# Attention and experts in one kernel: one key row block copied by ScalarE, fewer zero fills, and weight and row-part transfers issued from ScalarE's queue

## The chip, the cores and the metric

One core of a Trainium2 chip runs the whole program. The metric is the device time of one execution in microseconds, taken as the median over several runs. The engines are named as in the profile: PE (TensorE), DVE (VectorE), ACT (ScalarE), POOL (GpSimd) and SP (SyncE, which here only issues DMAs). SPq and ACTq are the DMA-issuing instructions of SP and ACT.

## The reference

A layer normalised input goes through latent attention (16 heads of 8 content and 32 rotary columns, 16 batches of 256 tokens) and, beside it, through a mixture of 8 experts with the two best taken, and a shared expert. Both results are added to the input.

```
x  = L0_attn_x                      # 16 x 256 x 128, float32
xn = layernorm(x)
kv = rmsnorm(xn @ W_kv) * g_kv;  q_c = xn @ W_q
k  = [kv @ W_kdec, rope(xn @ W_krope)];  v = kv @ W_vdec
q  = [q_c @ W_qdec, rope(q_c @ W_qrope)]           # 16 heads x 40 columns
attn = softmax(causal(q k^T / sqrt(40))) v @ W_o
probs = softmax(xn @ Wg);  two best of 8, renormalised
ffn  = sum over the two of (silu(xn @ W1[e] + b1[e]) @ W2[e] + b2[e]) * weight
       + 0.1 * (silu(xn @ Ws1 + bs1) @ Ws2 + bs2)
out  = x + attn + ffn
```

## The kernel before, in words

**Two phases.** In the first, `run_turns` runs turns b = -3 to 16 on every engine, each of `STEPS` = 16 steps. A turn works on several batches at once: it projects and turns batch b+2, takes the row maxima of b and b+1, the final scores, exponentials and values of b, and finishes b-1. What is done at which step stands in hand-written tables (`PROJ_AT`, `TURNED_AT`, `MROWS_AT`, `PV_AT` and others), so each engine's order is fixed, and semaphores tie the engines together. Turns 1, 5, 9 and 13 also hold a router group of eight tiles, whose work lies mostly on DVE. In the second phase `expert_out`, `hidden` and their partners run 31 passes of 512 rows: two shared ones, 23 routed blocks, six shared ones.

**High and low parts.** Products are taken in float32r with each operand split in a rounded high part and the rest. The queries and keys of a head are therefore stacked three times in `QK`: 3 blocks of `D` = 40 partitions. `part_heads` (ACT, L802) copies a turned bank to `heads_high` (keys: steps 15, 0, 2 and 3), `take_low` (DVE, L1099) writes the low part, and SP's `restack` (L482) copies both by DMA, 40 partitions at a time, to the right block of `QK`: for each batch 2 sides x 3 head groups x 3 blocks = 18 copies, all at L494. Key group 0 is wanted first, by `scores_for_max` of the next batch's head 0 (PE L1529, at step 9).

**Row maxima.** `put_max` (ACT, L821 and L823) copies the turned maxima of eight heads to `mT` and places them by a small DMA in two more partitions of `QK`. It is issued at step 3 for heads 0 to 7, which `head_scores` (PE L1439) begins at step 6, and at step 11 for heads 8 to 15, begun at step 14.

**Expert weights.** In turns 0 to 8 (`weights_at`) one expert's weights a turn are split by POOL (`split_weights`, steps 8 and 11) and then, from SP's queue, stored in two DMAs of 512 KB (L517), and the next ones are loaded in two of 256 KB (L476, L477). SP also stores each batch's turned and split rows, `xn_parts`, 256 KB (L502). SP's `turn` is in this order: rows of b+2, `restack` of b+1 (keys 0 and 1, queries 2, keys 2), weights, `restack` of b+2 (queries 0 and 1).

**Fills.** After the turns, SP clears 512 rows behind each expert's last row, and 7 more blocks that stand for unused routed blocks: `FILLS` = 15 DMAs of 256 KB (L566), then waits for them and for the scattered rows before it loads block rows (L549). SP gets there while the other engines are still in turn 15.

## Time and profile before

| | |
|---|---|
| runs | 743.53 us median of 3 (740.61 to 744.3) |
| profiled execution | 746.28 us, span 744.1 us |
| PE, PEld busy | 633.1, 511.8 us |
| DVE, ACT, POOL busy | 568.2, 391.5, 356.8 us |
| mean granted TensorE clock | 0.944 of 2.4 GHz |

The span is from the first to the last instruction; 2.2 us lie around it. Issuing a DMA is not counted as busy. A turn is told below by POOL's instruction at L742, which runs once a turn at its step 1: the stretch called turn b begins with it. In the rows by stretch stand, for each engine, busy us and (x) instructions in the order PE, PEld, DVE, ACT, POOL, then the granted TensorE clock as a share of 2.4 GHz (1.00 is that level, 0.50 would be 1.2 GHz), the busy share of the 16 DMA engines and GB/s.

### The profile page before, as it was taken

Reading aid. Unit: us, or ns where it says so; the run is one execution under the profiler, and the core shown is the slowest. Engines: PE = TensorE matmul, PEld = TensorE weight load, DVE = VectorE, ACT = ScalarE, POOL = GpSimd, SP = SyncE. Lnnn points to the kernel's source line nnn. Section 1 sums busy time; section 2 is a strip of 40 time slices with the busy share of each in tenths; the row PEclk is TensorE's granted clock in tenths of the full one; section 3 lists DMA queues with packets and bytes.
Section 4 is the critical chain, followed back from the end, with each engine's and each line's share of the span. In section 5 each row is a group of like instructions: output and inputs, shape, how many; then the busy total and the mean of one; then the engine's idle time right before and its main releaser. Section 6 shows DMA issues by size and latency. Waiting matters only on the chain.

```text
span 744.1 us, 14766 instructions
## 1 busy us (share of the span) xinstructions
PE 633.1 (85%) x4646; PEld 511.8 (69%) x4646; DVE 568.2 (76%) x1456; ACT 391.5 (53%) x842; POOL 356.8 (48%) x460
## 2 busy tenths in 40 slices
PE   2668878989887888988799998777799999999995
PEld 1457657767666766766677776665578888888884
DVE  5667798867688877678978878883757777789896
ACT  1323535535453554554455655433477777777773
POOL 7526454775754667466355455332300000457673
PEclk9877999989998999999999999988989999999998
DMA  7344655656566565655444555458625877889753
GB/s 195 111 161 162 205 171 194 210 186 202 185 207 202 168 197 183 219 201 178 130 156 168 165 173 173 130 159 257 210 94 174 257 249 247 265 288 307 223 173 86
DMA packets 66285, 141.66 MB, mean 190 GB/s; under 512 B 9204, under 2 KB 34849, under 8 KB 66209
## 3 DMA queue, kind: packets, MB, share of 16 engines
q1 hardware_dynamic: 61005, 131.36, 54.7%
q0 software_dynamic: 4096, 8.40, 4.1%
q10 hardware_dynamic: 1108, 0.97, 0.4%
q8 instruction: 38, 0.62, 0.3%
q14 instruction: 38, 0.31, 0.1%
HBM read 47.30 MB, written 29.88 MB: 104 GB/s over the span
## 4 chain that ended last, share of the span: by engine, by line
PE 51%; DVE 15%; POOL 10%; issue 9%; DMA 8%; SPq 5%; ACT 2%; POOLq 0%; DVEq 0%; ACTq 0%
PE bank L1692 9%; DMA QK<-mT 5%; PE bank L1710 5%; POOL QK L778 4%; PE bank L1440 4%; PE bank L1515 3%; PE bank L1456 3%; PE bank L1529 3%; SPq L494 3%; PE bank L1532 3%; PE bank L1442 3%; PE bank L1714 3%; DVE mx L1089 3%; DVE rot L1064 2%; PE bank L1563 2%
## 5 line engine op out<-in xcount | busy, mean ns | idle before, releaser
L1089 DVE TENSOR_REDUCE mx<-bank 128x3 f32<-128x384 f32 x256 | 141.8, 554 | 76.5 <-PE bank L1532 74.3
L834 ACT ACTIVATE prob<-bank 128x384 f32<-128x384 f32 x256 | 125.2, 490 | 134.7 <-PE bank L1442 132.9
L675 POOL TENSOR_TENSOR rot<-rot,t 128x512 f32<-128x512 f32 x64 | 82.1, 1283 | 138.6 <-DVE t L1079 138.5
L778 POOL DMA_INDIRECT QK<-expert_outs,out_at x64 | 65.6, 1025 | 139.3 <-DMA expert_outs<-prob 121.0
L1529 PE MATMUL bank<-QK 120*128 120x256 f32 x256 | 97.8, 382 | 31.8 <-issue 21.5
L1383 DVE TENSOR_TENSOR QK<-vaug,QK 128x512 fp32r<-128x512 f32 x124 | 86.5, 699 | 40.8 <-ACT QK L930 38.2
L1440 PE MATMUL bank<-QK 122*128 122x256 f32 x256 | 88.3, 345 | 0.0
L1439 PE MATMUL bank<-QK 122*128 122x128 f32 x256 | 76.1, 297 | 10.2 <-DMA QK<-mT 9.8
L758 POOL DMA_INDIRECT expert_rows<-xn,place_of x64 | 67.5, 1055 | 32.7 <-PE bank L1442 22.4
L1515 PE MATMUL bank<-ident,rot 128*120 128x128 f32 x384 | 69.5, 295 | 13.4 <-DVE heads_low L1099 8.1
L1529 PEld LDWEIGHTS bank<-QK 120*128 120x128 f32 x256 | 54.5, 213 | 36.4 <-issue 24.1
L811 ACT ACTIVATE heads_high<-bank 120x384 fp32r<-120x384 f32 x96 | 47.1, 494 | 58.3 <-PE bank L1515 51.2
L1532 PE MATMUL bank<-mask_qk,identb 128*128 128x256 bf16 x256 | 76.5, 299 | 0.0
L1442 PE MATMUL bank<-identb,mask_qk 128*128 128x256 bf16 x256 | 75.3, 294 | 0.0
L1099 DVE TENSOR_TENSOR heads_low<-bank,heads_high 120x384 fp32r<-120x384 f32 x96 | 52.8, 553 | 20.8 <-ACT heads_high L811 19.4
L1692 PE MATMUL bank<-heads_high,wb 128*128 128x512 f32 x276 | 68.6, 397 | 0.0
L924 ACT ACTIVATE vaug<-bank,xn 128x512 f32<-128x512 f32 x92 | 63.0, 687 | 2.5 <-PE bank L1692 0.5
L1515 PEld LDWEIGHTS bank<-ident,rot 128*120 128x120 f32 x384 | 47.0, 147 | 24.4 <-DVE heads_low L1099 11.0
L1439 PEld LDWEIGHTS bank<-QK 122*128 122x128 f32 x256 | 51.3, 200 | 16.8 <-DMA QK<-mT 13.5
L1530 PE MATMUL bank<-QK 120*128 120x128 f32 x256 | 59.3, 232 | 0.0
L1692 PEld LDWEIGHTS bank<-heads_high,wb 128*128 128x128 f32 x276 | 50.1, 188 | 9.3
L1530 PEld LDWEIGHTS bank<-QK 120*128 120x128 f32 x256 | 52.4, 205 | 0.1
(229 smaller groups left out, 1465.1 us busy)
## 6 DMA issues: line engine op xcount, KB each, us to landing
QK<-heads_high SPq DMA_DIRECT2D x96, 200.0 KB
wb<-weight_parts SPq DMA_DIRECT2D x35, 512.0 KB, 4.7
QK<-heads_high SPq DMA_DIRECT2D x48, 240.0 KB
QK<-heads_low SPq DMA_DIRECT2D x48, 200.0 KB
weight_parts<-wb SPq DMA_DIRECT2D x18, 512.0 KB, 5.8
QK<-queries_high SPq DMA_DIRECT2D x32, 200.0 KB
rot<-expert_rows SPq DMA_DIRECT2D x23, 256.0 KB, 4.2
expert_outs<-prob SPq DMA_DIRECT2D x23, 256.0 KB, 4.5
```

The lines of the kernel that those rows point to most:

```text
L778: nc.gpsimd.indirect_dma_start(out=gy[:, t, k, :], out_offset=None, in_=outs_d[0:READY[q] * SLOTS, :], in_offset=bass.IndirectOffsetOnAxis ...
L834: act_f(prob[:, h % P_SLOTS, :], ST_PS[h % 2][:, P:4 * P], ACT.Exp, scale=SCALE).then_inc(s_exp, 1)
L1089: V.tensor_reduce(mx[:, 0:3, h], B_PS[bank_of(k)][:, 0:3 * P].rearrange("p (a c) -> p a c", a=3), AX.X, ALU.max).then_inc(s_bfree[bank_of( ...
L1383: V.tensor_tensor(aparts[:, m % 2, 1, c, :], act[c], high, ALU.subtract).then_inc(s_alo, 1)
L1439: mm(ps[:, P:T], k[:, P:T], q[:, P:T], start=True, stop=False, skip_group_check=True)
L1440: mm(ps[:, T:2 * T], k[:, 0:P], q, start=False, stop=False, skip_group_check=True)
L1442: mm(diag, mask_qk[:, :], identb[:, :].unsqueeze(1).to_broadcast([P, 2, P]), start=False, stop=True, skip_group_check=True).then_inc(s_st, 1)
L1515: ins = nc.tensor.transpose(B_PS[bank_of(k)][0:KQ, g * P:(g + 1) * P], rows[:, at:at + KQ], ident[:, :])
L1529: mm(ps[:, 0:T], q[:, P:T], kk, start=True, stop=False, skip_group_check=True)
L1530: mm(ps[:, T:T + P], q[:, 0:P], kk[:, 0:P], start=False, stop=False, skip_group_check=True)
L1532: mm(diag, identb[:, :], mask_qk[:, :].unsqueeze(1).to_broadcast([P, 2, P]), start=False, stop=True, skip_group_check=True).then_inc(s_bfi ...
L1692: ins = mm(banks[c][:, :], w[:, part * F + c * P:part * F + (c + 1) * P], xT[m % 2][:, a, :], start=(i == 0), stop=(i == 2))
```

## The change

Four edits.

1. Block 0 of key group 0 is no longer copied by DMA. ACT writes it itself behind each of the four key copies of `part_heads` (steps 15, 0, 2, 3): it waits for its own copy and copies 40 partitions x 384 elements from `heads_high` to `QK`. `restack` of key group 0 then issues two DMAs, the high one and the low one. PE waits for `s_kd` as well.
2. The stores and loads of expert weights and the store of the row parts are issued from ACT's queue: stores at steps 12 and 15, loads at step 13 and at step 1 of the next turn, row parts at step 4, each behind everything else of its step.
3. Unused routed blocks read row 0 onwards in place of cleared rows of their own, so that 8 fills are left of 15. For it DVE has one more small instruction in `list_blocks`.
4. Before the fills SP waits until the last batch's second half of maxima is placed (`s_mrow[1]`).

```diff
+W_STORE_AT = {12: 0, 15: 1}
+W_LOAD_AT = {13: (0, 0), 1: (1, 1)}
+SEND_STEP = 4
...
-FULL = 2 * TILES * P // SLOTS
-ROWS = E * CAP + (NB - FULL) * SLOTS
-FILLS = E + NB - FULL
+ROWS = E * CAP
...
-                rows_of = ((0, high), (1, high), (2, low)) if side == "q" else ((0, high), (2, high), (1, low))
-                for row, part in rows_of:
-                    if i == 0 and row == rows_of[0][0]:
-                        sp.wait_ge(s_hi, raw_no(beta, 2 * n + 1, 1) + 1)
-                    if i == 0 and row == rows_of[2][0]:
+                rows_of = {"q": (0, 1, 2), "k": (0, 2, 1) if i else (2, 1)}[side]
+                if i == 0:
+                    sp.wait_ge(s_hi, raw_no(beta, 2 * n + 1, 1) + 1)
+                for row in rows_of:
+                    if i == 0 and row == rows_of[-1]:
                         sp.wait_ge(s_bfree[bank_of(k)], FREE_NO[k])
+                    part = low if row == rows_of[-1] else high
                     sp.dma_start(QK[row * D:(row + 1) * D, beta % 2, n, heads[0]:heads[-1] + 1, :].bitcast(F32),
-                                 part[i * D:(i + 1) * D, 0:len(heads), :].bitcast(F32)).then_inc(stacked(beta, side)[0][i], 16)
+                                 part[i * D:(i + 1) * D, 0:len(heads), :].bitcast(F32)).then_inc(stacked(beta, side, i)[0], 16)
...
-                if known(b + 2):
-                    sp.wait_ge(s_xh, b + 3)
-                    sp.wait_ge(s_xl, b + 3)
-                    sp.dma_start(parts_d[:, :, (b + 2) * T:(b + 3) * T].bitcast(F32),
-                                 xhl[:, par, :, :].bitcast(F32)).then_inc(s_xst[par], 16)
...
-                e = weights_at(b)
-                if e is not None:
-                    sp.wait_ge(s_whi, 2 * (e + 1))
-                    sp.wait_ge(s_wlo, 2 * (e + 1))
-                    for part in range(2):
-                        sp.dma_start(w_d[e, :, part, :].bitcast(F32), w_split[part][:, :].bitcast(F32)).then_inc(s_wst, 16)
-                    if e + 1 < NE:
-                        load_raw(e + 1)
...
+            sp.wait_ge(s_mrow[1], 16 * B)
+            for i in range(E):
...
+                if side == "k":
+                    heads = slice(half * TG // 2, (half + 1) * TG // 2)
+                    at_least(sc, s_st, (beta - 2) * H + HEADS_OF[0][-1] + 1)
+                    sc.wait_ge(s_hi, raw_no(beta, order, half) + 1)
+                    act_f(QK[0:D, beta % 2, 1, heads, j * P:(j + 1) * P], hs[0:D, 1, heads, j * P:(j + 1) * P],
+                          ACT.Copy).then_inc(s_kd, 1)
+            def store_weights(e, part):
+                sc.wait_ge(s_whi, 2 * e + part + 1)
+                sc.wait_ge(s_wlo, 2 * e + part + 1)
+                sc.dma_start(w_d[e, :, part, :].bitcast(F32), w_split[part][:, :].bitcast(F32)).then_inc(s_wst, 16)
+            def load_weights(e, part):
+                sc.wait_ge(s_wlo, 2 * e - 1 + part)
+                if part == 0:
+                    sc.dma_start(w_raw[:, 0:F], W1[e] if e < E else Ws1).then_inc(s_wl, 16)
+                else:
+                    sc.dma_start(w_raw[:, F:2 * F].rearrange("p (c h) -> p c h", c=FC),
+                                 (W2[e] if e < E else Ws2).rearrange("(c p) h -> p c h", p=P)).then_inc(s_wl, 16)
+            def send_parts(b, par):
+                sc.wait_ge(s_xh, b + 1)
+                sc.wait_ge(s_xl, b + 1)
+                sc.dma_start(parts_d[:, :, b * T:(b + 1) * T].bitcast(F32), xhl[:, par, :, :].bitcast(F32)).then_inc(s_xst[par], 16)
...
+                    if known(b + 2) and s == SEND_STEP:
+                        send_parts(b + 2, par)
+                    e = weights_at(b)
+                    if e is not None and s in W_STORE_AT:
+                        store_weights(e, W_STORE_AT[s])
+                    if s in W_LOAD_AT:
+                        back, part = W_LOAD_AT[s]
+                        e = weights_at(b - back)
+                        if e is not None and e + 1 < NE:
+                            load_weights(e + 1, part)
...
-                    steps.add(V.memset(shift[:, SEGS:SEGS + 1], float(E * CAP - FULL * SLOTS)))
+                    steps.add(V.memset(shift[:, SEGS:SEGS + 1], 0.0))
...
+                    steps.add(V.scalar_tensor_tensor(out=seg, in0=seg, scalar=float(SEGS), in1=block_no, op0=ALU.is_lt,
+                                                     op1=ALU.mult))
...
+                            pe.wait_ge(*stacked(beta, side, i))
+                if h == 0:
+                    pe.wait_ge(s_kd, 4 * (beta + 1))
```

## Rows read from the trace of the kernel before

**Rows 1.** Busy time by stretch: turns 1, 3+4, 5, 6, 7+8, 9, 11.

```profile
86.07:121.82 35.75, 28.25 (x237) 22.50 (x237) 31.02 (x87) 15.19 (x38) 16.16 (x22) 0.90 0.58 189
149.57:211.88 62.31, 54.29 (x456) 43.61 (x456) 44.08 (x123) 30.32 (x75) 39.00 (x51) 0.92 0.60 198
211.88:247.84 35.96, 28.26 (x237) 23.36 (x237) 31.65 (x87) 15.45 (x39) 19.80 (x26) 0.91 0.59 190
247.84:276.55 28.71, 25.05 (x228) 20.04 (x228) 22.23 (x62) 15.11 (x38) 19.37 (x27) 1.00 0.59 190
276.55:337.57 61.02, 53.09 (x456) 41.87 (x456) 44.91 (x123) 30.36 (x75) 38.98 (x51) 0.94 0.59 194
337.57:370.52 32.95, 27.46 (x237) 21.31 (x237) 28.75 (x87) 15.36 (x39) 15.12 (x22) 0.95 0.48 156
397.72:424.58 26.86, 24.80 (x228) 20.03 (x228) 21.37 (x62) 15.01 (x38) 14.85 (x22) 1.00 0.52 167
```

**Rows 2.** Timeline, SP's DMA issues, turn 7 (start us, us, what).

```profile
279.38 0.98 SPq L502 DMA_DIRECT2D xn_parts<-wb  x1
280.46 1.66 SPq L494 DMA_DIRECT2D QK<-heads_high  x2
...
283.63 4.06 SPq L494 DMA_DIRECT2D QK<-heads_high  x2
...
297.12 2.82 SPq L517 DMA_DIRECT2D weight_parts<-wb  x2
299.98 0.91 SPq L476 DMA_DIRECT2D xn<-in_L_ffn_Ws  x1
```

**Rows 3.** Timeline, SP's DMA issues, turn 11: first and last of twelve lines.

```profile
400.04 1.53 SPq L494 DMA_DIRECT2D QK<-heads_high  x2
...
423.07 0.72 SPq L494 DMA_DIRECT2D QK<-queries_low  x1
```

**Rows 4.** Timeline, PE, turn 11 (in brackets idle before and releaser).

```profile
402.94 0.30 PE L1439 MATMUL bank<-QK 122*128 122x128 f32 x1
...
407.92 0.36 PE L1529 MATMUL bank<-QK 120*128 120x256 f32 x1 [0.44 <-issue]
```

**Rows 5.** Timeline, ACT, turn 11, step 3.

```profile
398.68 0.62 ACTq L823 DMA_DIRECT2D QK<-mT  x1
```

**Rows 6.** Timeline, ACT, steps 15 and 0 of turns 11 and 12.

```profile
420.13 0.49 ACT L811 ACTIVATE heads_high<-bank 120x384 fp32r<-120x384 f32 x1 [1.12 <-PE bank L1515]
420.52 0.48 ACT L834 ACTIVATE prob<-bank 128x384 f32<-128x384 f32 x1
...
421.37 0.51 ACT L811 ACTIVATE heads_high<-bank 120x384 fp32r<-120x384 f32 x1
```

**Rows 7.** Timeline, DVE, step 0 of turn 12.

```profile
421.91 0.56 DVE L1099 TENSOR_TENSOR heads_low<-bank,heads_high 120x384 fp32r<-120x384 f32 x1
```

**Rows 8.** Timeline, POOL, turn 7, the second half of the split.

```profile
295.77 1.28 POOL L721 TENSOR_TENSOR wb<-xn,wb 128x512 fp32r<-128x512 f32 x1
```

**Rows 9.** Chain of waits that ended last (start us, us, what).

```profile
48.62 5.98 DMA QK<-heads_low
...
508.31 7.14 DMA QK<-mT
...
523.99 2.98 DMA QK<-mT
...
540.54 5.22 PE bank L1692 x12
```

**Rows 10.** Busy time by stretch, two stretches of turn 15.

```profile
501.73:505.75 4.02, 3.94 (x40) 3.10 (x41) 2.70 (x10) 2.01 (x5) 1.75 (x2) 1.00 0.28 75
515.50:521.80 6.30, 6.29 (x38) 4.67 (x38) 1.59 (x3) 1.96 (x4) 1.75 (x2) 0.53 0.91 274
```

**Rows 11.** Timeline, SP's DMA issues, around the fills.

```profile
507.60 16.33 SPq L566 DMA_DIRECT2D expert_rows<-t  x15
532.00 0.37 SPq L549 DMA_DIRECT2D rot<-expert_rows  x1
```

More of the change, by code:

```diff
@@ L323, in build @@
         s_hi = sem("heads_high_ready")
+        s_kd = sem("keys_high_put")
         s_rk = {s: [sem(f"heads_{s}{i}_stacked") for i in range(3)] for s in ("q0", "q1", "k")}
@@ L438, in parts_of, with stacked @@
             return (hs_odd[:, :, :], ls_odd[:, :, :]) if beta % 2 else (hs[:, 0, :, :], ls[:, 0, :, :])
-        def stacked(beta, side):
-            return (s_rk["k"], 16 * 3 * (beta + 1)) if side == "k" else (s_rk[f"q{beta % 2}"], 16 * 3 * (beta // 2 + 1))
+        def stacked(beta, side, i):
+            if side == "k":
+                return s_rk["k"][i], 16 * (3 if i else 2) * (beta + 1)
+            return s_rk[f"q{beta % 2}"][i], 16 * 3 * (beta // 2 + 1)
         def side_of(order):
@@ L469, in _ @@
             sp.dma_start(braw[NE * FC + E:NE * FC + NE, :], bs2.rearrange("(a h) -> a h", a=1)).then_inc(s_wb, 16)
[L471 to L480 removed]
+            sp.dma_start(w_raw[:, 0:F], W1[0]).then_inc(s_wl, 16)
+            sp.dma_start(w_raw[:, F:2 * F].rearrange("p (c h) -> p c h", c=FC),
+                         W2[0].rearrange("(c p) h -> p c h", p=P)).then_inc(s_wl, 16)
             def restack(beta, side, i):
@@ L530, in _ @@
             for i in range(3):
-                sp.wait_ge(s_rk["k"][i], 16 * 3 * B)
+                sp.wait_ge(*stacked(B - 1, "k", i))
                 for n in range(2):
@@ L562, in _ @@
             sp.wait_ge(s_zero, 1)
-            for i in range(FILLS):
-                at = sp.value_load(fill_row[0:1, i:i + 1], min_val=0, max_val=ROWS - SLOTS) if i < E else \
-                    E * CAP + (i - E) * SLOTS
+            sp.wait_ge(s_mrow[1], 16 * B)
+            for i in range(E):
+                at = sp.value_load(fill_row[0:1, i:i + 1], min_val=0, max_val=ROWS - SLOTS)
                 sp.dma_start(rows_d[bass.ds(at, SLOTS), :].rearrange("(p i) c -> p i c", i=4),
@@ L570, in _ @@
             sp.wait_ge(s_tab, 1)
-            sp.wait_ge(s_fill, 16 * FILLS)
+            sp.wait_ge(s_fill, 16 * E)
             for r in range(2):
@@ L807, in part_heads @@
                 sc.wait_ge(s_bfill, k + 1)
-                landed, count = stacked(beta - 2 if side == "q" else beta - 1, side)
                 for i in range(3):
-                    at_least(sc, landed[i], count)
+                    at_least(sc, *stacked(beta - 2 if side == "q" else beta - 1, side, i))
                 act_f(parts_of(beta, side)[0][0:KQ, half * TG // 2:(half + 1) * TG // 2, j * P:(j + 1) * P], ps,
                       ACT.Copy).then_inc(s_hi, 1)
+                if side == "k":
+                    heads = slice(half * TG // 2, (half + 1) * TG // 2)
[18 more added lines that the diff above has]
+                sc.dma_start(parts_d[:, :, b * T:(b + 1) * T].bitcast(F32), xhl[:, par, :, :].bitcast(F32)).then_inc(s_xst[par], 16)
             def put_max(beta, half):
@@ L1255, in list_blocks @@
                     steps.add(V.tensor_copy(block_e[:, :], no))
-                    steps.add(V.scalar_tensor_tensor(out=row, in0=block_no, scalar=float(SLOTS), in1=row,
+                    steps.add(V.scalar_tensor_tensor(out=row, in0=seg, scalar=float(SLOTS), in1=row,
                                                      op0=ALU.mult, op1=ALU.add))
@@ L1525, in scores_for_max @@
                         for side in "qk":
-                            landed, count = stacked(beta, side)
-                            pe.wait_ge(landed[i], count)
+                            pe.wait_ge(*stacked(beta, side, i))
+                if h == 0:
+                    pe.wait_ge(s_kd, 4 * (beta + 1))
                 bank_free(k)
```

8 lines of the change are left out of this document (removed).

## The prediction

> **What bounds the kernel now.** I read the page's slices first, then busy time by stretch, then SP's and ACT's timelines, the chain of waits, and single timelines of PE, DVE and POOL. The second phase begins with PE's L1692 at 540.54 us and runs at one pace to the end [rows 9]. No edit touches its passes, so what matters is how soon it starts. In the first phase no engine is full. The reader is to see in [rows 1] that turns of equal work differ: turn 11, without weights, takes 26.86 us; turns 3 and 4 with them 62.31 together, turns 7 and 8 61.02, turn 6 28.71. PE runs 228 instructions in each. The router turns show the same: 35.75 and 35.96 us with weights, 32.95 without. In turns 3 and 4 ACT is busy for 30.32 us of 62.31 and POOL for 39.00, so neither is the bound. SP is: in turn 7 it issues without a pause. It reaches the keys' group 0 at 280.46, behind 0.98 us for the row parts, and has 2.82 us for the weight stores and 0.91 for the first of two loads still to come [rows 2]. In turn 11 twelve lines with 18 copies, from 400.04 to 423.79, hold 22.0 us of issue [rows 3], so that some 4 us of 26.86 stay free. A weight turn adds 2.82 + about 2 x 0.95 = 4.7 us and the wait for POOL's split, which ends at 297.05 [rows 8]: SP has no slack left, the copies come late, and PE waits for them at L1529. With these waits goes a lower granted clock of TensorE: 0.92 and 0.94 of 2.4 GHz in the weight turns, 1.00 in turn 11 [rows 1]. Turn 6 stands after a long router turn, in which SP caught up, and is nearly short; that is the best sign that SP's backlog, not the weights' own work, makes the others long.
>
> **Weights and row parts to ACT.** SP loses about 4.7 + 0.98 us and a wait a turn, and one copy of 0.8 (half of 1.66, [rows 2]): from some 29 us to 22. A weight turn should then go at the pace of turn 11 plus what ACT adds. ACT's own issue of the maxima takes 0.62 us [rows 5]; I take 0.62 for each new issue, between 0.37, SP's with nothing before it [rows 11], and 4.06 / 2 = 2.0 us, one of SP's longest pair [rows 2], because SP's long ones come behind its own unfinished copies and ACT has few. Five such issues are 3.1 us a turn. Those at steps 12, 13 and 1 lie in ACT's waits for PE, of which there are 1.12 us before the key copy alone [rows 6]; the one at step 4 lies ahead of an exponential that PE needs only two heads later. The one at step 15 is on the path: behind it in ACT's order stand step 0's exponential and the key copy at 421.37, and DVE's L1099 at 421.91 starts 0.03 us after that copy's end [rows 6, 7]. So +0.62. If the cover of the other four is gone, it is up to +2.5 more.
>
> **Block 0 on ACT.** Four copies more a turn, 64 in all. The exponential at 420.52 started 0.39 us behind the key copy of 0.49. The new copy first waits for that copy's end, so it costs about 0.49 in delay and 0.39 of its own less the 0.39 there was: +0.5 us each, 2.0 us a turn. Bounds: 0.4 and 0.9. The one at step 15 pushes the same key copy and L1099, +0.5 on the path. That at step 0 stands before the small products' copy, for which DVE is by then late itself; those at steps 2 and 3 stand before copies that PE uses only after values of the head group. I count those three at nothing, 1.5 us if uncovered. On the other side one DMA fewer before the first keys land gives 0.8 us, of which PE can use the wait it has: 0.44 at 407.92 [rows 4]. A turn without weights therefore comes to 26.86 + 0.50 - 0.44 = 26.92, one with them to 26.92 + 0.62 = 27.54.
>
> **The turns' sum.** Turns 3, 4, 7, 8: 62.31 + 61.02 - 4 x 27.54 = 13.2. Turn 6: 28.71 - 27.54 = 1.2. Router turns 1 and 5: 71.71 - 2 x (32.95 + 0.68) = 4.5. Turns 0 and 2 I leave. Together 18.8. Turns 9 to 14 lose 6 x 0.06 = 0.4. The same bytes now fall in less time: the DMA share of 0.60 over 30.7 us would be 0.67 over 27.5, against 0.52 in turn 11 [rows 1], and a transfer lands later the busier the engines are (2.98 us against 7.14 for the same maxima [rows 9]). For that I take 0.4 us off in each of nine turns, 3.6; the bounds are nothing and 1.5 a turn.
>
> **The start.** The chain runs through SP's issues to 48.62 and a landing of 5.98 us [rows 9]. One copy (0.8) and one row-part store (0.6 to 0.98) leave it: 1.5.
>
> **The fills.** SP starts 15 fills at 507.60 and needs 16.33 us, 1.09 each [rows 11]. Beside them the maxima of the last batch take 7.14 us to place, after them 2.98 [rows 9]. With the fills behind, I expect 2.98 there: 4.2 us sooner. Behind the long gap the clock was 0.53, and 38 matmuls took 6.30 us; 40 of the same steps took 4.02 at 1.00 [rows 10]. The gap shrinks to about 1.1 us, so 2.3 more. One copy fewer in batch 15 gives 0.8. Together 7.3. The 8 fills then start at 523.99 + 2.98 = 526.97, take 8.7 us and land near 539.7; block rows were loaded at 532.00 [rows 11] and would be 8 us later. PE first turns them behind the first shared pass, which starts at 540.54 and takes 5.2 [rows 9], so 539.8 plus a landing of 4.2 (the page's median) is in time by some 1.7 us. The small DVE instruction in the list of blocks and the cheaper clears I count at nothing: DVE has 5 us of slack a turn.
>
> **The sum.** 18.8 - 0.4 - 3.6 + 1.5 + 7.3 = 23.6 us, from the profiled execution's 746.28 (span 744.1): 722.7. The median of the runs is 743.53, 2.75 lower, and I expect the same of the new kernel: 720.
>
> **A rule against it.** ACT issues no large transfer in the turns now, so no row here shows two full queues. The Trainium skill, "DMA: Bandwidth & Descriptors", section "Issuing engines are not separate DMA queues", says that DMAs started from several engines share the same 16 DMA engines and that only the issuer's own time is saved, which is usually small. By it alone the 18.8 would be nothing and the time about 739 (746.28 - 4.8 - 2.75); the row of turn 7, with SP issuing all the time, speaks for issue time being what is short here. Its section "Queues, rings and completion order" says that each issuer's queue is consumed in order, which is the mechanism of rival 1.
>
> **Rivals.**
> 1. *The maxima stand behind the weights in ACT's queue.* The step-3 maxima are issued at 398.68 and PE's step-6 matmul runs at 402.94, 4.26 us later, without a wait [rows 4, 5]. New in the same queue are 512 KB at step 15 and 256 KB at step 1, five and two us before. At half of 194 GB/s [rows 1] 768 KB need 7.9 us, so 2.7 us are left ahead of the maxima; with a landing of 4 that is 2.4 us late in each of nine turns, 21.6 us in place of the 3.6 above. It speaks for it that such a transfer was slowed to 7.14 us beside the fills; against it, that nothing says that the two queues share evenly. Time: 743.53 - (23.6 + 3.6 - 21.6) = 738. Chance 0.2.
> 2. *The DMA engines, not SP's issue, are short.* SP's copies vary from 0.72 to 2.0 us [rows 2, 3], as if held back. Then weight turns stay near their length, ACT pays 1.1 us in nine of them, and 1.5 + 7.3 - 0.4 - 9 x 1.12 = -1.7 us remain: about 745. Against it turn 6, with the same bytes in 28.71. Chance 0.08.
> 3. *Slower: ACT waits for POOL.* Step 12's store waits for the split's first half and step 15's for the second; behind them in ACT's order stand the exponentials, and PE behind those. POOL ended the second half 20.5 us into turn 7 (297.05 - 276.55), and ACT's key copy of step 15 lies 22.4 us into turn 11 (420.13 - 397.72, [rows 6, 8]): 1.9 us of cover at least, and more, since the slow turn delayed POOL too. If a late load or store holds the split, each us past the cover counts nine times: 2.6 us past it eat the 23.6, and at 3.3 the time is 750. Chance 0.07.
>
> **How the numbers follow.** My forecast has 0.65. Its own range, 710 to 730, has at the low end no contention and a clock of 1.00 in all weight turns (3.6 + about 5), at the high end 1 us more in each of nine turns. The range of 8 in 10 reaches to rival 1: 710 to 739. A measurement of this kernel tells 0.5%, 3.7 us, from no change. The forecast and three parts in four of rival 1, whose 5.6 us are close to that bound, are faster; the rest of it and rival 2 are the same; rival 3 is slower: faster 0.80, same 0.13, slower 0.07.
>
> **What the profile would show.** Right: SP idle in every turn; weight turns at 27 to 28.5 us, clock near 1.00; ACT's new issues near 0.62 us; no wait at L1529; the maxima of batch 15 placed in 3 us; 8 fills behind them and PE's L1692 without a wait for rows. Wrong: PE waiting at L1439 at step 6 of weight turns (rival 1); SP's copies longer than before with PE still waiting at L1529 (rival 2); ACT waiting for POOL's L721 (rival 3).

## The result, and the profile of the changed kernel

The changed kernel takes 737.41 us (median of 20 runs), the kernel before 743.88 (20 runs). The ratio is 0.989, 95% interval 0.987 to 0.991: 1.1% faster, some 6 to 8 us, where 23.6 were forecast. Four of the 20 executions fell in a slower state (one took 844.0 us at a granted clock of 0.657); the ratio leaves them out, and without them the median is 736.2. The profiled execution has 737.71 us with a span of 735.5; PE is busy for 633.3 us, DVE 565.6, ACT 419.3, POOL 356.5, and the mean granted clock is 0.951.

The view by stretch of the changed kernel, the same turns as [rows 1] and with the same columns:

```profile
85.46:119.79 34.33, 27.74 (x237) 21.74 (x237) 30.89 (x87) 17.21 (x44) 16.14 (x23) 0.95 0.52 167
148.50:205.91 57.41, 51.67 (x456) 41.21 (x456) 43.94 (x123) 33.78 (x84) 38.72 (x52) 0.97 0.63 202
205.91:242.85 36.94, 31.27 (x237) 24.37 (x237) 30.61 (x87) 17.22 (x44) 19.80 (x26) 0.82 0.52 167
242.85:271.38 28.53, 25.18 (x228) 20.11 (x228) 22.22 (x62) 16.90 (x43) 19.38 (x27) 1.00 0.64 194
271.38:329.48 58.10, 52.01 (x456) 41.05 (x456) 43.99 (x123) 33.75 (x84) 38.73 (x51) 0.97 0.62 197
329.48:362.94 33.46, 27.64 (x237) 21.38 (x237) 28.66 (x87) 16.94 (x44) 15.09 (x23) 0.95 0.45 141
391.54:419.99 28.45, 26.27 (x228) 20.93 (x228) 21.29 (x62) 16.77 (x42) 14.81 (x22) 0.94 0.48 151
```

Turns 3 and 4 fell from 62.31 to 57.41 us and turns 7 and 8 from 61.02 to 58.10, not to 55.08. Turns 5, 9 and 11 became longer. Set against the forecast, from the two profiled executions (its 0.4 a turn for contention is put into the nine turns):

| part | forecast, us gained | measured |
|---|---|---|
| start, up to turn 0 | 1.5 | 3.5 |
| turns 0 and 2 | -0.8 | -3.8 |
| router turns 1 and 5 | 3.6 | 1.4 - 1.0 = 0.4 |
| turns 3 and 4 | 6.4 | 4.9 |
| turn 6 | 0.8 | 0.2 |
| turns 7 and 8 | 5.1 | 2.9 |
| turns 9 to 12 | -0.2 | -3.9 |
| turn 13 to the end | 7.2 | 4.4 |
| sum | 23.6 | 8.6 |

What the forecast said of SP came true. This is SP's timeline in turn 7, to be read beside [rows 2]:

```profile
270.05 1.57 SPq L492 DMA_DIRECT2D QK<-heads_low  x1
273.79 0.72 SPq L492 DMA_DIRECT2D QK<-heads_high  x1
274.55 0.73 SPq L492 DMA_DIRECT2D QK<-heads_low  x1
275.33 3.43 SPq L492 DMA_DIRECT2D QK<-heads_high  x2
```

SP stands idle from 271.62 to 273.79, and the last copy of the keys' group 0 has been issued 3.9 us into the turn (275.28 - 271.38), where it was 7.0 before (283.59 - 276.55). PE's waits for DMAs, the changed kernel first and the kernel before second (line, cause, us in total, times, longest); L1554 and L1529 are the same line of the code, and so are L1463 and L1439:

```profile
PE bank L1463 <- DMA QK<-mT: 6.2, 3, 3.1
PE bank L1554 <- issue: 2.6, 2, 1.4
PE bank L1554 <- DVE heads_low L1121: 0.4, 1, 0.4
```

```profile
PE bank L1529 <- issue: 21.5, 15, 3.8
PE bank L1439 <- DMA QK<-mT: 9.8, 7, 5.3
PE bank L1529 <- DVE heads_low L1099: 1.6, 2, 1.3
```

The wait for keys fell from 23.1 us to 3.0, as forecast, and yet only 8.6 us came out of it. Two questions follow: which edit removed it, and what took the other 11.5 us.

### The profile page after: what moved, and what is told of

It reads as the page before. It is cut to its first block, busy times and chain, and to the rows that moved or that the text cites. A ratio compares the mean times of both kernels' runs of the same rounds, so it can differ in the third digit from the quotient of the medians.

```text
span 735.5 us, 14889 instructions
## 1 busy us (share of the span) xinstructions
PE 633.3 (86%) x4646; PEld 507.4 (69%) x4646; DVE 565.6 (77%) x1457; ACT 419.3 (57%) x906; POOL 356.5 (48%) x460
## 4 chain that ended last, share of the span: by engine, by line
PE 48%; DVE 19%; issue 8%; POOL 7%; ACT 6%; DMA 5%; SPq 5%; ACTq 1%; POOLq 0%; DVEq 0%
PE bank L1717 10%; PE bank L1735 6%; DVE mx L1111 4%; PE bank L1480 3%; PE bank L1739 3%; SPq L492 3%; DVE rot L1086 3%; ACT heads_high L795 2%; PE bank L1539 2%; PE bank L1464 2%; DMA QK<-mT 2%; POOL QK L763 2%; DMA QK<-heads_low 2%; PE bank L1588 2%; ACT heads_out L853 2%
## 5 line engine op out<-in xcount | busy, mean ns | idle before, releaser
L845 ACT ACTIVATE prob<-bank 128x384 f32<-128x384 f32 x256 | 122.6, 486 | 120.1 <-PE bank L1466 117.5
L1554 PE MATMUL bank<-QK 120*128 120x256 f32 x256 | 96.8, 378 | 9.8 <-DVE mx L1111 6.7
L1539 PE MATMUL bank<-ident,rot 128*120 128x128 f32 x384 | 67.3, 288 | 15.8 <-DVE heads_low L1121 8.0
L1463 PE MATMUL bank<-QK 122*128 122x128 f32 x256 | 75.2, 294 | 6.6 <-DMA QK<-mT 6.2
L795 ACT ACTIVATE heads_high<-bank 120x384 fp32r<-120x384 f32 x96 | 46.8, 488 | 47.8 <-PE bank L1539 42.3
L1539 PEld LDWEIGHTS bank<-ident,rot 128*120 128x120 f32 x384 | 45.1, 143 | 27.2 <-DVE heads_low L1121 10.9
L1554 PEld LDWEIGHTS bank<-QK 120*128 120x128 f32 x256 | 53.9, 211 | 12.5 <-DVE mx L1111 7.9
L1463 PEld LDWEIGHTS bank<-QK 122*128 122x128 f32 x256 | 50.4, 197 | 13.6 <-DMA QK<-mT 7.8
L1464 PEld LDWEIGHTS bank<-QK 122*128 122x128 f32 x256 | 50.9, 199 | 1.1
```

Source lines behind the costliest of these rows:

```text
L845: act_f(prob[:, h % P_SLOTS, :], ST_PS[h % 2][:, P:4 * P], ACT.Exp, scale=SCALE).then_inc(s_exp, 1)
L1463: mm(ps[:, P:T], k[:, P:T], q[:, P:T], start=True, stop=False, skip_group_check=True)
L1464: mm(ps[:, T:2 * T], k[:, 0:P], q, start=False, stop=False, skip_group_check=True)
L1539: ins = nc.tensor.transpose(B_PS[bank_of(k)][0:KQ, g * P:(g + 1) * P], rows[:, at:at + KQ], ident[:, :])
L1554: mm(ps[:, 0:T], q[:, P:T], kk, start=True, stop=False, skip_group_check=True)
```

## The experiments

Every ratio is to the kernel before on the same chip. e1, e2, e4 and e5 ran on a chip where the kernel before took 767.5 us, the others where it took 743.5 to 744.8, so whole times in us are not compared across. The difference lies in the second phase: it lasts 222 to 226 us in the traces of these four and 203 to 204 in all others, while the lengths of turns are alike. Turns are therefore compared across chips below, each from one trace.

| kernel | what it is | ratio | interval |
|---|---|---|---|
| e2 | edit 1 alone | 0.991 | 0.987 to 0.996 |
| e3 | edit 2 alone | 1.011 | 1.006 to 1.015 |
| e4 | edits 3 and 4 alone | 0.999 | 0.995 to 1.003 |
| e1 | all but edit 1 | 1.006 | 1.001 to 1.011 |
| e12 | all but edit 2 | 0.987 | 0.982 to 0.991 |
| e6 | changed kernel again | 0.992 | 0.989 to 0.996 |
| e13 | edit 2, weights only | 0.998 | 0.994 to 1.001 |
| e14 | edit 2, row parts only | 1.007 | 1.004 to 1.010 |
| e16 | edit 2, row parts at step 1 | 1.000 | 0.997 to 1.003 |
| e8 | e1, row parts at step 1 | 1.000 | 0.997 to 1.003 |
| e5 | changed, block-0 copies later | 0.981 | 0.975 to 0.987 |
| e7 | changed, split a step later | 0.986 | 0.983 to 0.989 |
| e9 | changed, second phase's loads later | 0.984 | 0.981 to 0.988 |
| e10 | changed, all four moves | 0.971 | 0.967 to 0.975 |
| e11 | e10, weight stores later | 0.981 | 0.977 to 0.985 |
| e15 | e10 without edit 2 | 0.964 | 0.960 to 0.967 |

### The edits one by one

**e1, all but edit 1.** Block 0 goes back to a DMA.

```diff
-                rows_of = {"q": (0, 1, 2), "k": (0, 2, 1) if i else (2, 1)}[side]
+                rows_of = {"q": (0, 1, 2), "k": (0, 2, 1)}[side]
-                    act_f(QK[0:D, beta % 2, 1, heads, j * P:(j + 1) * P], hs[0:D, 1, heads, j * P:(j + 1) * P],
-                          ACT.Copy).then_inc(s_kd, 1)
```

> The changed kernel with its first edit undone: block 0 of key group 0 is again copied by SP's DMA, the transfers stay on ACT's queue and there are 8 fills. Theory A (ACT's four copies in the dense steps 15 to 3 push DVE's L1121 and the pair maxima 0.5 us back, the longer PE gap behind them brings the granted clock down in some turns, and together that took most of the expected gain): turns 10 and 11 back from 28.5 to about 27 us, L1554 waits again for about 0.4 us a turn, 724 to 729 us, ratio to before 0.973 to 0.981. Rival B (the copies are harmless; the transfers on ACT's queue or the DMA engines hold the weight turns at 28.4): 736 to 742 us, ratio 0.99 to 1.0.

**e2, edit 1 alone,** in the kernel before.

```diff
-                rows_of = ((0, high), (1, high), (2, low)) if side == "q" else ((0, high), (2, high), (1, low))
+                rows_of = {"q": (0, 1, 2), "k": (0, 2, 1) if i else (2, 1)}[side]
+                    act_f(QK[0:D, beta % 2, 1, heads, j * P:(j + 1) * P], hs[0:D, 1, heads, j * P:(j + 1) * P],
+                          ACT.Copy).then_inc(s_kd, 1)
```

> The kernel before with the first edit alone: block 0 of key group 0 written by ACT. Theory A: turns without weights 1 to 1.5 us longer, weight turns shorter by the 0.8 us that SP saves; in sum 742 to 750 us, ratio 0.998 to 1.01. Rival B: the removed copy pays in every turn, 733 to 740 us, ratio 0.985 to 0.995.

**e3, edit 2 alone,** in the kernel before.

```diff
+W_STORE_AT = {12: 0, 15: 1}
+W_LOAD_AT = {13: (0, 0), 1: (1, 1)}
+SEND_STEP = 4
...
-                        sp.dma_start(w_d[e, :, part, :].bitcast(F32), w_split[part][:, :].bitcast(F32)).then_inc(s_wst, 16)
...
+                        send_parts(b + 2, par)
...
+                        store_weights(e, W_STORE_AT[s])
...
+                            load_weights(e + 1, part)
```

> The kernel before with the second edit alone: weight and row-part transfers issued from ACT's queue, 15 fills, all key copies by DMA. The prediction's main term was 18.8 us for this edit and the copies together. From e1 (1.006 with the fills' edits) and e4 (0.999): theory F (the row parts at step 4 collide with the copies of key group 0, and the relief of SP is taken back by it) gives 1.002 to 1.010. Rival: SP's relief does pay alone, 0.98 to 0.99.

**e4, edits 3 and 4 alone.**

```diff
-FILLS = E + NB - FULL
+            sp.wait_ge(s_mrow[1], 16 * B)
+            for i in range(E):
```

> The kernel before with the fills' edits alone: 8 in place of 15, behind the last maxima. The prediction's term: 6.5 us less, of it 4.2 by the maxima placed sooner and 2.3 by the clock: 737 us, ratio 0.991. If the maxima are as late as in the changed kernel's chain (one placement of 4.97 us), only 2 to 4 us: 740 to 742 us, ratio 0.994 to 0.997.

**e12, all but edit 2:** weights and row parts stay with SP.

```diff
-W_STORE_AT = {12: 0, 15: 1}
-W_LOAD_AT = {13: (0, 0), 1: (1, 1)}
-SEND_STEP = 4
+            def load_raw(e):
```

> The changed kernel without its second edit: key block 0 on ACT, 8 late fills, transfers on SP's queue as before. Measured so far: copies alone 0.991, fills alone 0.999, all together 0.989 to 0.992. If the edits add up, 0.990, and the second edit is worth nothing; if the second edit is worth much once the copies are on ACT (its collision is then covered), 0.995 or more.

**What was measured.** Edit 1 alone brings 0.9% and edit 2 alone costs 1.1%. Without edit 2 the kernel has 0.987, with it 0.989 and 0.992: the edit that was to bring most of the gain brings nothing. Nearly the whole shortening of the weight turns is edit 1's. With it alone (e2) turns 3 and 4 are as short as in the changed kernel:

```profile
147.94:205.09 57.15, 51.41 (x456) 41.16 (x456) 43.70 (x123) 33.32 (x84) 38.69 (x52) 0.97 0.64 202
```

Turns 7 and 8 take 57.80 us there, and in e12 the two pairs take 57.97 and 57.74. The ratios of e1, 1.006, and of e4, 0.999, lie outside both of the ranges expected for them, and on the slow side. The trace of e3 shows which step of the forecast falls. These are SP's waits for the keys' high part, before and then in e3 (line, cause, us in total, times, longest):

```profile
SPq L491 <- ACT heads_high L811: 20.5, 8, 3.5
```

```profile
SPq L489 <- ACT heads_high L797: 46.8, 18, 4.6
```

SP is relieved: it now stands waiting for the keys 18 times, 46.8 us in all. PE's waits in e3, where L1546 is the matmul that wants keys and L1457 the one that wants maxima:

```profile
PE bank L1546 <- issue: 16.1, 12, 3.7
PE bank L1457 <- DMA QK<-mT: 11.9, 9, 3.7
...
PE bank L1546 <- DVE heads_low L1117: 5.4, 6, 2.2
```

PE waits for keys 21.5 us with SP relieved and 23.1 without. Turns 3 and 4 take 61.20 us in e3 and turns 7 and 8 60.78, against 62.31 and 61.02. So SP's backlog was there, but relieving it did not make the weight turns short. One reason is that SP's copies became slower. The source view of the copies gives the shortest, middle and longest issue in ns, for the kernel before and then for e3:

```profile
L494 SPq DMA_DIRECT2D QK<-heads_high x144: 717/1410/2342, 26.6 to 496.4; - x144
L494 SPq DMA_DIRECT2D QK<-heads_low x72: 717/1002/2040, 28.3 to 498.0; - x72
```

```profile
L494 SPq DMA_DIRECT2D QK<-heads_high x144: 717/1514/2250, 25.5 to 499.7; - x144
L494 SPq DMA_DIRECT2D QK<-heads_low x72: 717/1122/2734, 27.2 to 501.3; - x72
```

An issue takes 0.1 us longer with the same bytes on two queues; over 18 copies that is 1.8 us of the 4.7 to 5.7 freed in a weight turn. That is the sign named for rival 2, SP's copies longer and PE still waiting at the keys.

### The two halves of edit 2

**e13, only the weights on ACT's queue,** against e3:

```diff
+                    sp.dma_start(parts_d[:, :, (b + 2) * T:(b + 3) * T].bitcast(F32),
+                                 xhl[:, par, :, :].bitcast(F32)).then_inc(s_xst[par], 16)
...
-                    if known(b + 2) and s == SEND_STEP:
-                        send_parts(b + 2, par)
```

**e14, only the row parts,** against the kernel before:

```diff
+SEND_STEP = 4
...
-                    sp.dma_start(parts_d[:, :, (b + 2) * T:(b + 3) * T].bitcast(F32),
-                                 xhl[:, par, :, :].bitcast(F32)).then_inc(s_xst[par], 16)
...
+                    if known(b + 2) and s == SEND_STEP:
+                        send_parts(b + 2, par)
```

**e16, edit 2 with the row parts at step 1,** against e3:

```diff
-SEND_STEP = 4
+SEND_STEP = 1
```

> The kernel before, with only the weights' stores and loads on ScalarE's queue (steps 12, 13, 15 and 1); row parts stay with SyncE at the start of its turn. All of edit 2 alone had a ratio of 1.0106. Theory R (the row parts at step 4 are what costs, by the keys' copies they fall on): the wait for keys at head 0 in turns 10 to 12 is back at 0.44 to 0.5 us, those turns take 26.7 to 27.2 us, and the ratio is 0.995 to 1.000. Theory M (the weights in ScalarE's queue hold up the maxima): waits of 0.6 to 2.3 us for the placed maxima in four or more of turns 0 to 8, ratio 1.003 to 1.008. The prediction's own step (SyncE's issue is what weight turns lack) would have 0.985.

> The kernel before, with only the row parts' store on ScalarE's queue, at step 4; weights stay with SyncE. Theory R: the wait for keys at head 0 is 1.0 us in turns 10 to 12 (0.44 to 0.49 before), those turns take 27.6 us, 0.5 to 0.7 more in each of some 13 turns, ratio 1.006 to 1.011. Theory M: 0.998 to 1.003, since one transfer of SyncE's less frees 0.6 to 1.0 us of its issue in weight turns, which pays for it.

> Edit 2 alone, but with the row parts sent at step 1 in place of step 4. Theory R: the keys' wait in turns 10 to 12 is 0.4 to 0.5 us again, turns of 26.9, ratio 0.998 to 1.002. Theory M: the store now stands nearer to the maxima of step 3, whose waits in weight turns grow past 0.7 to 2.3 us; ratio 1.008 to 1.013.

Theory R, that the row parts at step 4 are what costs, holds. Alone they cost 0.7%, the weights alone move nothing that can be told (0.998), and with the row parts at step 1 the whole loss is gone (1.000). Turn 11 shows how, from three timelines of e14: SP's issues, ACT's, and PE's first matmul that wants the keys.

```profile
401.32 1.49 SPq L495 DMA_DIRECT2D QK<-heads_high  x2
402.86 1.13 SPq L495 DMA_DIRECT2D QK<-heads_low  x1
404.03 4.21 SPq L495 DMA_DIRECT2D QK<-heads_high  x2
```

```profile
402.00 0.59 ACTq L814 DMA_DIRECT2D xn_parts<-wb  x1
```

```profile
409.78 0.36 PE L1533 MATMUL bank<-QK 120*128 120x256 f32 x1 [1.04 <-issue]
```

The same in e13, where SP has sent the row parts 2.8 us ahead of the keys:

```profile
394.73 0.58 SPq L502 DMA_DIRECT2D xn_parts<-wb  x1
397.51 1.52 SPq L494 DMA_DIRECT2D QK<-heads_high  x2
399.08 1.00 SPq L494 DMA_DIRECT2D QK<-heads_low  x1
400.13 3.54 SPq L494 DMA_DIRECT2D QK<-heads_high  x2
```

```profile
405.41 0.36 PE L1549 MATMUL bank<-QK 120*128 120x256 f32 x1 [0.49 <-issue]
```

With 256 KB issued just ahead of the keys' low copy (402.00, the low copy 402.86), the low one's issue takes 1.13 us instead of 1.00, and the time from its end to PE's start 5.79 (409.78 - 403.99) instead of 5.33 (405.41 - 400.08). With it the wait doubles, from 0.49 to 1.04, in each turn without a longer wait. The waits for keys are 13.7 + 5.4 = 19.1 us in e13 and 26.1 + 0.8 = 26.9 in e14. Keys are not all of it: PE's wait for the placed maxima is 13.1 us in e14 as well, where it was 9.8 before.

Theory M, which is rival 1 (the maxima are held up by what else is in ACT's queue), shows too, in a smaller size: in turn 8 of e13 PE waited 1.97 us for maxima issued at 304.50 and used at 310.95, and 2.33 in turn 4 of e3. e14, with no weights in ACT's queue, has such waits as well. Up to turn 12, before the second phase's loads and the fills come into it, PE's waits for maxima add up to 1.6 to 2.8 us in the five traces in which ACT's queue holds only the maxima (before, e2, e4, e12, e15), and to 3.1 to 9.4 in the thirteen in which it also holds weights or row parts. So they go with ACT's queue. Whether it is the order in the queue or the moment of the transfer that does it, no run separates.

**e8, e1 with the row parts at step 1.**

```diff
-SEND_STEP = 4
+SEND_STEP = 1
```

> As e1_keys_by_dma (all key copies by DMA, transfers on ACT's queue, 8 fills), but the row parts' 256 KB issued at step 1 in place of step 4. In e1's turn 11 this store ran beside the copies of key group 0, PE's wait for them at L1546 was 1.05 us where it had been 0.44 and the maxima of step 11 were waited for 0.95 us. Theory F (the store at step 4 collides with the copies that PE waits for): turns without weights back from 28.5 to about 27 us, ratio to the kernel before 0.985 to 0.993 where e1 had 1.006. Rival: the wait has another cause, ratio 1.003 to 1.009.

It goes from 1.006 to 1.000, 0.6 points where it was 1.1 between e3 and e16 and 0.7 in e14, all with intervals of 0.3 to 0.5 either way; turns 10 to 12 fall from 28.6, 28.5 and 28.1 to 26.7, 27.3 and 27.3 us. In the changed kernel itself edit 1 covers the collision at the keys: with block 0 written by ACT there is no wait for keys from turn 0 to 12, even beside the row parts (in e6 one, of 0.42 us); no run moves the row parts alone in that kernel. The ratio of e8 is worse than the 0.985 to 0.993 expected: without edit 1, the relief of SP gains nothing even with the row parts out of the way.

### What took the rest

**e6, the changed kernel again.** No edit.

> The changed kernel itself once more, beside the others of this call. 0.989 of the kernel before, as measured first, if the chip makes no difference; turns without weights at 27.0 us where the granted clock is 1.00 and 28.5 where it falls to 0.94.

0.992, against 0.989 of the first series. Its turns 10 to 12 took 28.5, 27.1 and 27.1 us where the profiled execution above has 28.6, 28.5 and 27.1: the turns at a granted clock of 0.94 are 1.3 to 1.5 us longer than those at 1.00. Turn 11 differs between the two executions of one kernel, but turn 10 does not, and the traces of all runs together show a pattern. With edit 1 turn 10 is at 0.94 in nine of ten traces (not in e9), without it in one of eight (e14). Turns 9 to 12 take 116.9 us in e2 and 116.6 in e12, against 113.7 before and 113.0 in e13. So the loss there comes with edit 1, not with the transfers.

**e7, POOL's split one step later.**

```diff
-SPLIT_AT = {8: 0, 11: 1}
+SPLIT_AT = {9: 0, 11: 1}
```

> The changed kernel with POOL's first half of the weight split moved from step 8 to step 9, behind the parting of the maxima. In the trace DVE's pair maxima of step 9 take 1.16 us in weight turns and 0.16 in the others, and end with POOL's L704. Theory D (POOL's split holds up DVE's small SBUF operation, 1.0 us on the path in each of nine weight turns, and this is why these turns cannot reach 27): weight turns about 1 us shorter, L1131 at 0.16 us throughout, 726 to 730 us on the first chip's scale, ratio to the changed kernel 0.985 to 0.99. Rival E (weight turns are held by the DMA engines, so that a wait elsewhere takes the us back): ratio to the changed kernel 0.997 to 1.003.

In turn 8 of the changed kernel DVE's maximum over a pair of tiles, 128x8, takes 1.16 us instead of 0.16. DVE, POOL and PE around it:

```profile
312.31 1.16 DVE L1131 TENSOR_TENSOR mx<-mx 128x8 f32<-128x8 f32 x1
```

```profile
312.39 1.05 POOL L704 TENSOR_TENSOR wb<-xn,unit 128x512 fp32r<-128x512 f32 x1
```

```profile
314.42 0.36 PE L1593 MATMUL bank<-wkv,ksT 96*128 96x256 f32 x1 [1.13 <-DVE t L1101]
```

It ends at 313.47, 0.03 us behind POOL's copy at 313.44, and PE waits for what DVE does next. All eight stretched ones of this trace (0.62 to 1.31 us, turns 0 and 2 to 8) end 0.02 to 0.04 us behind an operation of POOL's split. The view by tile of this line, changed kernel and e7 (shortest, middle, longest ns):

```profile
L1131 DVE TENSOR_TENSOR mx<-mx x32: 154/157/1307, 54.2 to 514.0; 128x8 f32<-128x8 f32 x32
```

```profile
L1131 DVE TENSOR_TENSOR mx<-mx x32: 155/158/167, 54.8 to 511.8; 128x8 f32<-128x8 f32 x32
```

With POOL a step later none of 32 is stretched, and the ratio is 0.986, 0.6% below e6, though the two intervals just touch. The Trainium skill, "SBUF — State Buffer", section "Who interferes with whom", says that a VectorE instruction with two SBUF inputs contends with a GpSimd one that reads SBUF, over a port pair that is an exclusive lock, and that the order of issue decides which of the two blocks. These rows agree, but for the order: DVE's record starts 0.08 us ahead of POOL's, and DVE is the one held up. The stretched maximum was there before the change too, and not hidden: in the kernel before six of them took 0.60 to 1.23 us, and PE waited 0.70 to 0.93 us behind each, 5.0 in all. In the changed kernel there are eight, with waits of 0.60 to 1.28, some 8 in all. So only some 3 us of it took back part of the gain; the rest is a cost that was always there.

**e5, the block-0 copies out of steps 15 and 0 to 3.**

```diff
+PUT_AT = {4: 2, 7: 3}
...
-                if side == "k":
...
+                    if known(b + 1) and s in PUT_AT:
+                        put_keys(b + 1, PUT_AT[s])
```

> The changed kernel with ACT's four copies moved behind the work of steps 4 and 7, where ACT waits 2.6 and 2.1 us for PE: same copies, same number of DMAs. Theory A: pair maxima of step 1 back by 0.5 us a turn, clock near 1.00 in turns 10 and 11, no wait at L1554 of more than a few tenths; 722 to 728 us, ratio 0.970 to 0.979. Rival C (it is the load of 64 more instructions on ACT, wherever they stand, that costs): 735 to 740 us, ratio 0.988 to 0.995.

The copies cost what was forecast. ACT, changed kernel, step 15 of turn 11, beside [rows 6]:

```profile
415.09 0.49 ACT L795 ACTIVATE heads_high<-bank 120x384 fp32r<-120x384 f32 x1 [1.12 <-PE bank L1539]
415.67 0.52 ACT L801 ACTIVATE QK<-heads_high 40x384 fp32r<-40x384 f32 x1
416.10 0.47 ACT L845 ACTIVATE prob<-bank 128x384 f32<-128x384 f32 x1
```

```profile
417.45 0.56 DVE L1121 TENSOR_TENSOR heads_low<-bank,heads_high 120x384 fp32r<-120x384 f32 x1 [0.68 <-ACT heads_high L795]
```

From the first key copy to DVE's low part it is 417.45 - 415.09 = 2.36 us, and it was 421.91 - 420.13 = 1.78 [rows 6, 7]. Moved behind the work of steps 4 and 7, where ACT waits for PE anyway (2.56 and 2.10 us in turn 11 of the changed kernel), they are out of that chain, and the ratio is 0.981. The changed kernel had 0.989 to 0.992, but on other chips, so the size, some 0.8 to 1.1%, is less certain than the others. 0.970 to 0.979 had been expected.

**e9, the second phase's first loads behind the last batch's first maxima.**

```diff
             sp.wait_ge(s_pfill, B * PROJ_UNITS)
+            sp.wait_ge(s_mrow[0], 16 * B)
```

> The changed kernel with SP waiting for the last batch's first maxima before it loads the second phase's 2 MB (two shared weight parts, two row chunks). In the changed kernel these loads are issued at 499.3 to 501.5 and the maxima at 503.58 need 4.97 us. Theory G (they, not the fills alone, lie beside the maxima; the fills' removal could give only 2.2 of the expected 4.2 us): placed in about 3 us, phase two 2 to 4 us sooner, ratio to the changed kernel 0.994 to 0.998. Rival: 5 us is what a placement needs there, no change.

The chain of waits of the changed kernel, then of e9 (start us, us, step):

```profile
503.58 4.97 DMA QK<-mT
...
532.11 5.12 PE bank L1717 x12
```

```profile
505.23 2.24 DMA QK<-mT
...
530.45 5.26 PE bank L1718 x12
```

Edit 4 kept the fills from the maxima, as meant, but SP had issued 2 MB of the second phase's loads just before them. With these behind, the placing takes 2.24 us instead of 4.97, and the ratio is 0.984, 0.8% below e6, with intervals that do not overlap.

### Put together

**e10,** the changed kernel with e5, e7, e9 and the row parts at step 1.

```diff
-SPLIT_AT = {8: 0, 11: 1}
+SPLIT_AT = {9: 0, 11: 1}
-SEND_STEP = 4
+SEND_STEP = 1
+PUT_AT = {4: 2, 7: 3}
+            sp.wait_ge(s_mrow[0], 16 * B)
```

> The changed kernel with four moves together: ACT's key copies behind steps 4 and 7, row parts issued at step 1, POOL's first half of the split at step 9, and the second phase's loads behind the last batch's first maxima. Alone against the changed kernel they were about 0.992 (copies), 0.994 (split) and 0.992 (loads); if they add up, 0.970 to 0.975 of the kernel before, 722 to 725 us, with turns without weights at 26.5 us. If they hide one another, 0.978 to 0.984.

**e11,** e10 with the weights' store and load later.

```diff
-W_STORE_AT = {12: 0, 15: 1}
-W_LOAD_AT = {13: (0, 0), 1: (1, 1)}
+W_STORE_AT = {14: 0, 15: 1}
+W_LOAD_AT = {14: (0, 0), 1: (1, 1)}
```

> As e10_four_moves, with the first weight store and the first load at step 14 in place of 12 and 13. In e7, with the split out of the way, PE waited 0.47 us in turn 4 for the maxima issued at step 11, which needed 5.13 us beside the store issued 1.6 us behind them. Theory H (the store at step 12 is what the maxima of step 11 wait for next): 2 to 5 us less than e10, above all in turn 0. Rival 1 of the prediction (maxima stand behind weights in ACT's queue): the maxima of step 3 now have 768 KB closer before them and come late, no gain or 2 to 8 us more.

e10 has 0.971, e11 0.981: later is worse. In turn 6 of e11 ACT's timeline has

```profile
265.00 0.35 ACTq L815 DMA_DIRECT2D weight_parts<-wb  x1
265.39 1.78 ACTq L821 DMA_DIRECT2D xn<-in_L_ffn_W  x1
267.27 0.49 ACT L852 ACTIVATE prob<-bank 128x384 f32<-128x384 f32 x1 [1.95 <-PE bank L1475]
267.51 1.67 ACTq L815 DMA_DIRECT2D weight_parts<-wb  x1
267.66 0.49 ACT L798 ACTIVATE heads_high<-bank 120x384 fp32r<-120x384 f32 x1
269.29 0.49 ACT L852 ACTIVATE prob<-bank 128x384 f32<-128x384 f32 x1 [1.14 <-PE bank L1475]
```

The same 512 KB store whose issue takes 0.35 us elsewhere (265.00, and the middle one of the changed kernel's) takes 1.67 close behind other large transfers, ACT's next exponential starts only at 269.29, and PE waits 0.95 us for what follows it (turns 0, 2, 3, 4, 6 and 7 each have such a wait, of 0.7 to 0.95, and in e10 none reaches 0.4). This is the cover lost that the prediction priced at up to 2.5 us a turn.

**e15, e10 without edit 2:** weights and row parts from SP, as in the kernel before. Against e12:

```diff
-SPLIT_AT = {8: 0, 11: 1}
+SPLIT_AT = {9: 0, 11: 1}
+PUT_AT = {4: 2, 7: 3}
+            sp.wait_ge(s_mrow[0], 16 * B)
```

> The kernel with the four moves (0.9711) with edit 2 undone: weights and row parts from SyncE's queue as before, the block-0 copies behind steps 4 and 7, the split at step 9, and the second phase's loads behind the first maxima stay. If SyncE's relief is worth nothing in any company: 0.968 to 0.974, weight turns 27 to 28.5 us. If it pays once the other waits are gone (it frees 5.7 us of issue in a weight turn): 0.978 to 0.984, with waits for keys of 0.5 to 1 us in weight turns. The sum of the parts measured alone (0.9866 without edit 2, 0.8 points for the copies' place, 0.6 for the split, 0.8 for the loads) is 0.965.

0.964, 718.7 us: the fastest of all, and ahead of e10 (0.971), if by little (the intervals touch). By stretch, turns 3 and 4, and 7 and 8 of e15:

```profile
144.64:202.54 57.90, 49.50 (x456) 40.20 (x456) 42.73 (x123) 33.37 (x83) 38.70 (x51) 1.00 0.63 202
263.18:319.82 56.64, 51.44 (x456) 41.00 (x456) 42.64 (x123) 33.48 (x83) 38.71 (x51) 0.97 0.63 202
```

Waits for keys are 8.2 + 0.8 us at 7 places here and 4.4 + 0.2 at 3 in e10, so SP's relief does shorten them once other waits are out of the way (turns 3 and 4: 56.41 us in e10), but not the kernel. What it gives there it takes at the maxima. PE's waits for them, e15 first and e10 second:

```profile
PE bank L1457 <- DMA QK<-mT: 3.0, 7, 0.7
```

```profile
PE bank L1472 <- DMA QK<-mT: 7.3, 9, 2.1
```

Keys and maxima together are 12.0 us in e15 and 11.9 in e10. 0.964 is below both ranges expected, and the sum of the parts was 0.965. The second phase begins at 515.47 in e15 and at 514.80 in e10, 0.7 us apart. The traced execution is the longest of e15's six and the shortest of e10's, so the 3.7 us between the medians lie in executions that were not traced.

## Why the prediction was wrong, step by step

**SP's backlog makes the weight turns long, and its relief brings them to the pace of turn 11 (18.8 us): the step that failed.** The backlog was real and the relief came, but the relief alone is worth -1.1% (e3), and nothing without the row parts' collision (e13, e16). The weight turns of 3, 4, 7 and 8, forecast at 27.5 us each (27.9 with the 0.4 for contention), took 28.9 on average in the changed kernel, 30.5 with the relief alone (e3) and 28.7 with edit 1 alone (e2). What removed the wait for keys is edit 1: 5.1 us of it are left in e2, 5.7 in e12, 21.5 in e3. I had booked edit 1 at one copy, 0.8 us, and counted its use at PE with the 0.44 us of turn 11. One copy fewer is issued and 240 KB fewer lie ahead of the low part; which of the two does it, no run separates. Turn 6, which I took as the best sign, does not decide: it was 28.71 us with SP caught up, and is 28.53 after.

**The rule against it.** By the Trainium skill, "DMA: Bandwidth & Descriptors", section "Issuing engines are not separate DMA queues", the time was to be about 739; measured are 737.4, and e13 at 0.998 agrees with it in a single number. That the total comes so near is partly chance: turns 1 and 3 to 8 gained 8.4 us, by edit 1 (9.1 in e2), while turns 0, 2 and 9 to 12 lost 7.7. I named the rule, and let the row of turn 7 decide. A row that shows an issuer always busy shows that it has no slack. It doesn't show that PE's wait goes when slack is given.

**ACT's price of an issue.** Forecast 0.62 us each, measured 0.35 (stores), 0.33 to 0.39 (loads), 0.59 (row parts), the middle ones of each. The one on the path, at step 15, costs about 0.1 us instead of 0.62: from the key copy to the exponential it is 325.55 - 324.43 = 1.12 us in turn 8 with it and 416.10 - 415.09 = 1.01 in turn 11 without, since it runs beside the copy ahead of it (325.10 beside the copy of 325.02 to 325.55).

**Block 0's price.** Forecast +0.5 us on the path, measured 2.36 - 1.78 = 0.58. Turn 12 at a clock of 1.00 takes 27.08 us, forecast 26.92. Right on the path, with one thing left out: turns 10 and 11 ran at 0.94 and took 28.6 and 28.45, and with them turns 9 to 12 lost 3.9 us for the 0.2 forecast. e2 and e12 lose 3.2 and 2.9 there too, so this term of edit 1 was put too low; the forecast looked for a higher clock in weight turns only, and for no fall in the others.

**The clock of weight turns.** It rose, from 0.92 and 0.94 to 0.97 in both pairs, if not to the 1.00 forecast. It fell in turn 5, to 0.82 with 36.94 us for 35.96, and e6 has the same again (36.92 us at 0.82).

**What ends last once the keys are early** was not asked. One part is DVE's maximum beside POOL's split, 1.0 to 1.3 us of PE's waiting in turns 0, 2, 4, 5, 6 and 8 and 0.6 in turns 3 and 7, which e7 removes. It could have been read beforehand: the chain of waits of the kernel before has this line five times with 0.99 us, beside the same two operations of POOL.

**Rival 1** came late and small. In the traced execution of the changed kernel the maxima of turn 0 were issued at 71.08 and used at 77.30, and PE waited 2.88 us, but the store of 512 KB (72.72) and the load (73.77) stood behind them in the queue. In turns 3 to 8 there is no such wait of 0.4 us or more, where 2.4 a turn were feared; e6, the same kernel, has one of 1.31 in turn 8. Once ACT's copies are out of the way, the form that was feared is there: PE waits for the step-3 maxima, in the first 8 us of a turn, 6.1 us in turns 1 to 7 of e5 and 5.6 in turns 1 to 9 of e10, and 0.4 in e15, whose weights go from SP's queue. It is what e10 pays for the relief of SP. That the measured time lies within the wide range, 710 to 739, is luck: the range reached so far for 21.6 us of this rival, of which a few came, and the forecast's own, 710 to 730, missed. **Rival 2** is nearest to what happened, for edit 2 by itself: SP's issues 0.1 us longer, PE still waiting. **Rival 3** did not come; ACT has no wait for POOL's L706.

**The start** gained 3.5 us, not 1.5: PE's first wait for keys fell from 3.83 to 1.23 us, again edit 1 (1.59 in e2, 3.69 in e3). **The fills:** eight in 9.94 us from 519.63, and PE did not wait for block rows, as forecast; but the maxima took 4.97 us and not 2.98, and the second phase began 8.4 us earlier (532.11 against 540.54), of which 4.2 had been gained before turn 13. Alone, edits 3 and 4 are 0.999: in the trace of e4 the same maxima still took 6.11 us, from 507.62, with the second phase's loads just ahead of them, and from turn 13 to the second phase it is 88.5 us where it was 89.3. Beside edit 1 they show more, 83.4 us in e12 against 89.7 in e2. The step that failed in this term is that the fills alone made the placing slow: e9 shows what the loads had in it.

**Still open.** By what edit 1 brings the clock of turn 10 down is not settled, nor why turn 11 or 12 falls in one execution and not in the next; e5, with the copies moved, still had 0.94 in two of turns 10 to 12. Together, such turns are a few us either way. That edit 2 takes something back from edit 1 is not shown either: the intervals of e12 and of the changed kernel overlap, and those of e15 and e10 touch.

## What to carry to other kernels

A queue that issues without a pause is a suspect, not a verdict: ask what the waiting engine would still wait for if that queue were free, and look at the last transfer of the chain, its bytes and its neighbours. Taking one transfer out of the chain by a small copy on an engine (0.5 us) was worth more than moving five large ones to another queue. After removing a wait, list what was ready less than a microsecond before it ended, and what the moved work now stands beside: here the placing of the maxima, a stretched 0.16 us instruction and a 256 KB store at the wrong step took back part of what the edits had won.
